# Side work of VectorE inside a step of a Mamba scan: eight SiLU products and sixteen token-shift mixes per chunk move from a step's end to its middle

## What is computed

```
x = x + 0.5 * ffn(layernorm(x));  x = x + mamba(layernorm(x));  x = x + 0.5 * ffn(layernorm(x))

ffn(x):    xr = mu_r*x + (1-mu_r)*x_prev;  xk = mu_k*x + (1-mu_k)*x_prev       # the "mixes"; x_prev: the token before
           return sigmoid(xr @ W_r) * (relu(xk @ W_k)**2 @ W_v)

mamba(x):  xs, z = split(layernorm(x, ln_w, ln_b) @ W_in.T)                    # 1024 channels each
           xc = silu(b_conv + sum over k of 4 of xs shifted by 3-k, times W_conv[:, k])
           dt_low, B, C = split(xc @ W_xproj.T)                                # 32, 16 and 16 columns
           delta = softplus(dt_low @ W_dt.T + b_dt)
           h_t = exp(delta_t * A) * h_(t-1) + delta_t * B_t * xc_t             # 1024 channels x 16 states
           y_t = sum over the 16 states of h_t * C_t
           return ((y + D_skip*xc) * silu(z)) @ W_out.T + x
```

## Time and profile before

| | |
|---|---|
| median of 3 runs | 5426.3 us (5424.6 to 5429.3) |
| profiled execution: its own time, its span | 5428.4 us, 5426.3 us |
| VectorE busy | 4967.8 us, 92% |
| TensorE busy | 4474.0 us, 82%, mean granted clock 0.905 of full |
| ScalarE busy | 3031.2 us, 56% |
| GpSimd busy | 2906.2 us, 54% |
| VectorE's scans (L1065), 2048 of 1279 ns each | 2619.8 us |
| VectorE's idle time in front of scans, released by ScalarE's decay | 171.0 us |

### The profile page before, as it was taken

The page is one execution under the profiler, slowest core; times in us unless marked ns, Lnnn a source line. Parts: engine busy times, 40 slices in busy tenths (PEclk is TensorE's granted clock), DMA queues, the critical chain, the costliest instruction groups (busy, mean ns, idle before and its releaser), DMA issues.

```text
span 5426.3 us, 59521 instructions
## 1 busy us (share of the span) xinstructions
PE 4474.0 (82%) x16640; PEld 2497.0 (46%) x16640; DVE 4967.8 (92%) x5826; ACT 3031.2 (56%) x6291; POOL 2906.2 (54%) x2111
## 2 busy tenths in 40 slices
PE   6677888888888878888888888878888788888788
PEld 2344544444454444545444444444544444444443
DVE  2899999999999999999999999999999999999993
ACT  2555655555555555555556555555655656555552
POOL 1545556465565545555455564555555455554661
PEclk9878999898999989999998989989999898998888
DMA  1545555454554545555455554556556565554651
GB/s 64 154 122 166 156 164 157 124 173 142 172 154 149 156 137 168 157 155 164 131 165 152 171 155 140 155 139 171 154 149 169 135 168 155 168 154 117 168 162 64
DMA packets 423066, 810.80 MB, mean 149 GB/s; under 512 B 41264, under 2 KB 41264, under 8 KB 418640
## 3 DMA queue, kind: packets, MB, share of 16 engines
q1 hardware_dynamic: 422736, 807.00, 52.0%
HBM read 772.25 MB, written 34.60 MB: 149 GB/s over the span
## 4 chain that ended last, share of the span: by engine, by line
DVE 49%; PE 22%; issue 16%; ACT 8%; DMA 2%; POOL 2%; DVEq 1%; SPq 0%; POOLq 0%; ACTq 0%
DVE decay L1065 22%; DVE g L1075 13%; PE mm L420 5%; DVE xc L1019 4%; PE y_acc L504 4%; PE mm L431 4%; PE mm L446 3%; PE mm L409 2%; PE mm L527 2%; DVE xc L1029 2%; PE mm L456 2%; DVE mix_k L996 2%; ACT rows L662 2%; DMA res_scratch<-rows 2%; DVE xn_col L1001 2%
## 5 line engine op out<-in xcount | busy, mean ns | idle before, releaser
L1284 POOL TENSOR_TENSOR dbx<-u,b_all 128x1024 f32<-128x1024 f32 x1024 | 2413.5, 2360 | 2131.8 <-DVE decay L1065 2130.6
L1065 DVE TENSOR_TENSOR_SCAN decay<-decay,state,dbx 128x512 f32<-128x512 f32 x2048 | 2619.8, 1279 | 172.6 <-ACT decay L849 171.0
L504 PE MATMUL y_acc<-ident,g 128*128 128x128 f32 x8192 | 1220.3, 291 | 372.5 <-DVE g L1075 359.6
L849 ACT ACTIVATE decay<-delta,neg_a 128x512 f32<-128x512 f32 x2048 | 1415.5, 692 | 68.4 <-ACT state L855 0.4
L504 PEld LDWEIGHTS y_acc<-ident,g 128*128 128x128 f32 x8192 | 1005.6, 149 | 922.9 <-DVE g L1075 578.8
L1075 DVE TENSOR_TENSOR g<-decay,c_all 128x512 f32<-128x512 f32 x2048 | 1374.9, 671 | 7.6 <-PE y_acc L504 7.6
L855 ACT ACTIVATE state<-decay 128x1 f32<-128x1 f32 x2048 | 340.6, 167 | 1519.3 <-DVE g L1075 1517.5
L431 PE MATMUL mm<-wbuf_c,col 128*128 128x512 f32 x1024 | 459.9, 593 | 0.9 <-DVE rows L1008 0.9
L409 PE MATMUL mm<-mix_k,wbuf_c 128*128 128x512 f32 x512 | 293.4, 728 | 118.2 <-ACT col L727 76.8
L446 PE MATMUL mm<-xn_col,wbuf_a 128*128 128x512 f32 x512 | 302.1, 746 | 68.4 <-ACT delta L808 48.5
L446 PE MATMUL mm<-xn_col,wbuf_d 128*128 128x512 f32 x512 | 290.4, 720 | 72.2 <-ACT col L727 70.5
(11 more groups left out here) (92 smaller groups left out, 4557.8 us busy)
## 6 DMA issues: line engine op xcount, KB each, us to landing
b_all<-bc_scratch SPq DMA_DIRECT2D x1024, 256.0 KB, 3.8
c_all<-bc_scratch SPq DMA_DIRECT2D x1024, 256.0 KB, 4.5
wbuf_c<-in_w_v SPq DMA_DIRECT2D x32, 1024.0 KB, 7.8
wbuf_d<-in_w_r SPq DMA_DIRECT2D x16, 1024.0 KB, 6.7
xin<-in_x SPq DMA_DIRECT2D x16, 1024.0 KB, 10.3
wbuf_c<-in_w_k SPq DMA_DIRECT2D x16, 1024.0 KB, 8.2
wbuf_d<-in_w_in SPq DMA_DIRECT2D x16, 1024.0 KB, 7.5
wbuf_a<-in_w_in SPq DMA_DIRECT2D x16, 1024.0 KB, 10.4
```

Of the source, the lines that this page charges most:

```text
L504: last = pe.matmul(y_acc[:, tb, j * P:(j + 1) * P], g[:, m % GRING, tb * P:(tb + 1) * P], ident[:, :], start=n == 0 and j == 0 and tb % 2 ...
L849: act.activation(decay[:, m % DBANKS, :], delta[:, q % 2, j, :], ACT.Exp, scale=neg_a[:, QT * q + j, n:n + 1]).then_inc(decay_done, 1)
L1065: dve.tensor_tensor_scan(d, d, dbx[:, s % DBX, j, :], state[:, batch, m:m + 1], ALU.mult, ALU.add).then_inc(scan_done, 1)
L1284: pool.tensor_tensor(dbx[:, s % DBX, :, :], u[:, q % 2, :, :], b_all[:, s % BRING, :].unsqueeze(1).broadcast_to([P, QT, W]), ALU.mult).the ...
```

## The change

It is VectorE's order that changes. The same instructions run, with the same operands. A block of side work is inserted in front of scan(2s+1): the mixes of ffn 0 keep their steps (4, 5, 7, 8) and move to the middle of them; the SiLU product of tile e moves from the end of step 33+2e to the middle of step 34+2e; the mixes of ffn 1 move from the ends of steps 35, 37, 40, 41 to the middles of 37, 39, 41, 43, two in each. The names of the semaphore counts of `m_dve` follow the new order. One wait is changed on ACT: `ffn_relu2` for tile j waits for the r mix of tile j instead of for the last of the four.

```diff
--- before.py
+++ after.py
@@ -147,7 +147,9 @@
                       "tap0 last0 tap1 last1 th0 tap2 last2 th1 tap3 last3 th2 tap4 last4 th3 "
                       "tap5 last5 th4 tap6 last6 th5 tap7 last7 th6 th7 xp")
         m_dve = Marks(sem("mamba_dve"), ["st0", "st1", "st2", "st3", "mv0", "mv1", "mv2", "mv3"]
-                      + [f"{q}{e}" for e in range(ET) for q in ("c0_", "c1_", "c2_", "head", "silu")])
+                      + ["c0_0", "c1_0", "c2_0", "head0"]
+                      + [q for e in range(1, ET) for q in (f"silu{e - 1}", f"c0_{e}", f"c1_{e}", f"c2_{e}", f"head{e}")]
+                      + ["silu7"])
         m_pool = Marks(sem("mamba_pool"), ["v", "v2"] + newton + ["mean", "shift", "one",
                        "h0", "h1", "h2", "h3", "h4"])
         h_pe = Marks(sem("quarter_pe"), "dt0_0 dt0_1 sk0 dt1_0 dt1_1 sk1 dt2_0 dt2_1 sk2 dt3_0 dt3_1 sk3")
@@ -722,7 +724,7 @@
             def ffn_relu2(i, k, j):
 
                 act.wait_ge(f_pe[i].sem, f_pe[i].at(k, f"k{j}"))
-                act.wait_ge(f_dve[i].sem, f_dve[i].at(k, "xr3"))
+                act.wait_ge(f_dve[i].sem, f_dve[i].at(k, f"xr{j}"))
                 o = col[:, j, 0:W]
                 act.activation(o, bank(f"f{i}k{j}"), ACT.Relu).then_inc(f_act[i].sem, 1)
                 act.wait_ge(f_act[i].sem, f_act[i].at(k, f"rel{j}"))
@@ -1087,6 +1089,22 @@
                             weigh(it, 2 * s - 1)
                     elif back:
                         weigh(b, NM - 1)
+
+                    if front and s in (4, 5):
+                        ffn_mix_k(0, f, 2 * (s - 4))
+                        ffn_mix_k(0, f, 2 * (s - 4) + 1)
+                    if front and s in (7, 8):
+                        ffn_mix_r(0, f, 2 * (s - 7), xn_col[:, other, :, :])
+                        ffn_mix_r(0, f, 2 * (s - 7) + 1, xn_col[:, other, :, :])
+                    if front and s in (34, 36, 38, 40, 42, 44, 46, 48):
+                        conv_silu(f, (s - 34) // 2)
+                    if back and s in (37, 39):
+                        ffn_mix_k(1, b, s - 37)
+                        ffn_mix_k(1, b, s - 36)
+                    if back and s in (41, 43):
+                        ffn_mix_r(1, b, s - 41, xin)
+                        ffn_mix_r(1, b, s - 40, xin)
+
                     if scn:
                         scan(it, 2 * s + 1, bt)
                         weigh(it, 2 * s)
@@ -1094,14 +1112,8 @@
                     if back and s == 3:
                         gate_y(b, 6)
                         gate_y(b, 7)
-                    if front and s in (4, 5):
-                        ffn_mix_k(0, f, 2 * (s - 4))
-                        ffn_mix_k(0, f, 2 * (s - 4) + 1)
                     if back and s in (6, 12, 23, 25):
                         out_add(b, (6, 12, 23, 25).index(s))
-                    if front and s in (7, 8):
-                        ffn_mix_r(0, f, 2 * (s - 7), xn_col[:, other, :, :])
-                        ffn_mix_r(0, f, 2 * (s - 7) + 1, xn_col[:, other, :, :])
                     if front and s in (17, 18, 20, 21):
                         ffn_gate(0, f, (17, 18, 20, 21).index(s))
                     if front and s in (19, 20, 22, 23):
@@ -1124,23 +1136,12 @@
                         gate_y(it, 1)
                     if front and s in (32, 34, 36, 38, 40, 42, 44, 46):
                         conv_taps(f, (s - 32) // 2)
-                    if front and s in (33, 35, 37, 39, 41, 43, 45, 47):
-                        conv_silu(f, (s - 33) // 2)
                     if scn and s == 34:
                         gate_silu(it, 2)
-                    if back and s in (35, 37):
-                        ffn_mix_k(1, b, s - 35)
-                        ffn_mix_k(1, b, s - 34)
                     if scn and s == 38:
                         gate_silu(it, 3)
                     if scn and s in (40, 42):
                         gate_y(it, s // 2 - 18)
-                    if back and s == 40:
-                        ffn_mix_r(1, b, 0, xin)
-                    if back and s == 41:
-                        ffn_mix_r(1, b, 1, xin)
-                        ffn_mix_r(1, b, 2, xin)
-                        ffn_mix_r(1, b, 3, xin)
                     if back and 55 <= s < 59:
                         ffn_gate(1, b, s - 55)
                     if ahead and s in (58, 59):
```

## The result

The changed kernel takes 5122.6 us (median of 4, 5121.5 to 5123.5) against 5425.6 (median of 4): a ratio of 0.944, 95% interval 0.9424 to 0.9457, 303 us less. The forecast was 5147 in 5090 to 5225.

The account below looks back on a forecast made before the run. VectorE was taken as the bound, busy 4967.8 of 5426.3 us. Per chunk 7.6 + 12.5 - 0.7 - 0.8 = 18.6 us, times fifteen 279, off 5428.4 gives 5149, stated as 5147; range 5090 to 5225.

Parts of the forecast that it names:

- What VectorE's instructions cost: VectorE's instructions with two SBUF inputs block until GpSimd's product ends; SiLU products fall from 2.50 to 0.72 us mid-step.
- Mixes of ffn 0: Steps 4, 5, 7, 8: three pairs of 3.25 us become 1.40, one of 5.32 becomes 1.46; 9.3 us a chunk.
- (a): ScalarE's chain in step 5, hidden before, makes scan 12 wait: minus 2.2 us a chunk; from step 36, minus 0.8.
- e = 0: First SiLU product of a chunk: no gain, since VectorE waited there anyway; its move costs 0.7 us.
- (b): TensorE after step 8: its fourth k group starts 6.2 us earlier, plus clock; 7.6 us taken for the front half.
- Mixes of ffn 1: Already at 770 ns; moving them gives 0 to 0.5 us, taken as 0.
- (c): Steps 35 to 47: 74 us for TensorE's 65.8, part at the lower clock; no loss taken.
- the rival that TensorE takes over: Steps 35 to 47: TensorE at the lower clock becomes the bound, half of 18.6 is left, 5288 us; 12 in 100.
- The meeting of tile 3 with u: GpSimd's u follows its product of step 43; 0.2 us decide, losing costs 36 us: 5183, counted within the main case.

Follow-up runs that it names:

- e5: The changed kernel with the moved block directly behind the first scan of the same step instead of in the middle: 5186.5 us.
- e7: The changed kernel with the moved block at the end of the same steps, behind the product with C: 5585.2 us.
- e11: The kernel before, with GpSimd's product computing only 256 of the 512 columns (result not valid, run for its time alone): 5209.0 us.
- e8: The changed kernel with ScalarE's four columns for the r mixes of ffn 0 in steps 6 and 7 instead of 5 and 6: 5100.2 us.
- e3: The kernel before with ScalarE's relaxed wait alone (the relu of tile j waits for r mix j): 5422.1 us.
- e4: The changed kernel, but the relu of ffn 0 waits for the last r mix again: 5121.7 us.
- e1: The kernel before with the eight SiLU products alone moved to the middles of steps 34 to 48; mixes and ScalarE's wait as before: 5320.5 us.
- e6: The changed kernel with the moved block directly behind the second scan of the same step, ahead of the product with C: 5327.6 us.
- e10: The changed kernel with some of ScalarE's mix columns for both ffns in later steps, and the SiLU products directly behind the second scan: 5097.2 us.

## Why the prediction was right

- **What VectorE's instructions cost.** Two prices, set by GpSimd: shown from VectorE's side by e5 to e7 (2576, 1392, 799 and 672 ns by place alone) and from GpSimd's by e11. The middle was priced at 0.72 us from start to start; the timeline has 0.73 (2490.26 to 2490.99). Busy time fell by 336 us, forecast about 330; the idle time before scans rose by 62 us, forecast 30 to 60.
- **Mixes of ffn 0**, forecast 9.3 us of blocked time a chunk: steps 4, 7 and 8 gave 1.84, 1.83 and 3.85, step 5 its 1.7 before scan 12's wait.
- **(a), ScalarE in step 5**, forecast 2.2: measured 1.94, and its mechanism shown by e8. The table load took 1.28 us and the softplus came 1.30 behind its start, as before. The Trainium skill (ScalarE: Activation LUTs, "What ACT_TABLE_LOAD costs") has 2.66 us for a switch, load and drain, which does not show here. The scans behind steps 35 and 37, forecast 0.8, waited 0.26 and 0.68, but the 0.68 is a mean of two kinds: at most 0.08 us in seven passes and 1.2 to 1.8 in six, all of them passes in which step 33 was short (see e = 0).
- **(b), TensorE after step 8**, taken at 7.6 in 6.9 to 8.7: the front half gave 8.9 (7.3 in steps 4 to 8, and 1.6 in steps 12 and 13), more than the upper bound. The sum was built rightly and one term of it was sized too small. The fourth k group:

```profile
2339.92 0.58 ACT L729 ACTIVATE col<-mm 128x512 f32<-128x512 f32 x1
...
2340.65 2.81 PE L411 MATMUL mm<-mix_k,wbuf_c 128*128 128x512 f32 x6 [0.88 <-ACT col L729]
```

These are six of its eight instructions; the view ends there. It starts 1.67 us after the start of step 9 where it started 0.91 after it, so 6.5 us earlier in the pass, forecast 6.2. All eight take 3.67 us instead of 6.02 in the mean: 2.4 us from the clock, of which the forecast had 0.7 to 2.5 in its range and 1.4 in its sum (7.6 less 6.2). 6.5 and 2.4 are the 8.9. The granted clock of steps 9 and 10, in the mean, went from 0.64 to 1.00, after a wait of 0.88 us instead of 5.36 in front of the group. e3 shows that the start alone does not do it.
- **e = 0**, forecast a loss of 0.7: steps 33 and 34 together got 0.6 us a chunk shorter. This term had the wrong sign. The second product with C of step 34 no longer waits 0.4 us for TensorE's sums, which pays for more than half of the moved product. The rest goes with TensorE's clock. Step 33 now ends with ScalarE's decay, which follows TensorE's xs group of step 32 (eight matmuls of the input projection): where that group takes 4.5 to 4.8 us from its first to its last start, step 33 takes 5.1 to 5.3, in seven of the 13 passes; where it takes 5.6 to 6.1 (6.1 is the lower level throughout), step 33 takes 6.2 to 6.7. In e4, which differs by one wait, no pass had the short group, and steps 33 and 34 were as long as before (13.6 us). Why the group differs is not settled. The time was the same within 1 us all the same, since what a short step 33 wins is lost again before the scan behind step 37: steps 33 and 37 take 11.4 us together in either trace. So the 0.6 is in part luck of the clock; taken with the waits of steps 35 and 37, both traces lose 0.3 us a chunk where the forecast lost 1.5.
- **Mixes of ffn 1**, forecast 0 to 0.5: right for the full change, 770 to 748 ns. But it was priced as a move that does nothing, and e1 shows that without it some 60 us of the gain stay away. The forecast read 770 ns as the price of a place where nothing collides, and did not ask what kept GpSimd away there. The full change comes out right because it moves these mixes too.
- **(c), TensorE in steps 35 to 47**, no loss: 60.5 us busy of 73.4, at 0.93. The stretch was forecast at 74, and the mean is 74.1. Two readings behind the rival that TensorE takes over were off, without bearing on the sum: the clock of the busy stretch in the earlier trace rows is 0.97 and not 0.96, and the group of 6.07 us has its last two instructions at the higher level already, so a group wholly at the lower would cost more.
- **The meeting of tile 3 with u**: decided by 0.22 us, in VectorE's favour, in all 15 passes. What was not seen is a small follower: the addition of the head in step 40 (L1025) now stands behind the next product of GpSimd in 15 passes, 0.45 instead of 0.16 us.

A mean pass fell from 327.5 to 307.0 us, 20.5, where 18.6 was forecast. The difference lies in (b), 1.3, and in e = 0, 1.3, less 0.7 in other places (0.3 of it the addition of the head).

## What to carry to other kernels

When one instruction of VectorE has two prices, look at what GpSimd runs at that moment before looking at its operands, and find the place in the loop that GpSimd leaves free: here a move of 1.8 us in time was worth 5.6%. Count the second in line too, since the first of a group pays for all; moving the one that pays leaves the bill to the next. Where GpSimd has two instructions in a row, work out who asks first to 0.2 us.

## What the runs showed of the hardware beyond that

- Who asks first goes first, and a queue has no hold on its place: a mix directly behind a mix lost its turn to a GpSimd product that had asked 0.27 us after the first mix began (e6, 60 pairs, 2.8 us each). The Trainium skill (SBUF — State Buffer, "Who interferes with whom") says that issue order decides who blocks. The traces agree, if the order is that in which the instructions ask: in the change the SiLU product of tile 3 asks 0.22 us before u and goes first, in e10 u asks 0.96 us before it and goes first.
- The wait does not shrink with the instruction: the addition of 128x3 (L1025), with both inputs in SBUF, stood for 0.45 instead of 0.16 us behind a GpSimd product.
- VectorE blocks GpSimd as well: u was recorded at 2.80 instead of 2.35 us when the SiLU product had the turn.
- A blocked instruction ended 0.54 to 0.55 us after GpSimd's, at whatever place it stood (before, change, e5, e10, e11), sooner than the 0.67 of a free one. That some of its time lies in the wait already would explain it; no run shows this.
